# Two graph layers over a symmetric 8192x8192 adjacency on one core: second-layer parts of two adjacent rows share one step, one bank and one addition, and the finished groups are staggered

## The reference

```
x_drop  = x * (u >= 0.1) / 0.9
x       = layernorm(x + adj @ x_drop)
x_proj  = tanh(|x|) * x / (|x| + 1e-8)              # |x| clipped to 10
s       = adj @ x_proj
out     = arctanh(|s|) * s / (|s| + 1e-8)           # |s| clipped to 0.999
x       = layernorm(x + out @ kernel + bias)
```

## Time and profile before

| | |
|---|---|
| median of 3 runs | 982.45 us (981.58 to 983.51) |
| the profiled execution | 981.5 us |
| its span, first to last instruction | 979.4 us |
| mean granted TensorE clock | 0.973 |
| TensorE, VectorE, ScalarE, GpSimd busy | 92%, 38%, 5%, 6% |
| loads of blocks | 330 of 1 MB, 353.12 MB moved in all |
| chain that ended last | TensorE 78%, DMA 7%, VectorE 5%, issue 4%, GpSimd 3% |

### The profile page before, as it was taken

The page is one execution under the profiler, slowest core; times in us unless marked ns, Lnnn a source line. Parts: engine busy times, 40 slices in busy tenths (PEclk is TensorE's granted clock), DMA queues, the critical chain, the costliest instruction groups (busy, mean ns, idle before and its releaser), DMA issues.

```text
span 979.4 us, 10731 instructions
## 1 busy us (share of the span) xinstructions
PE 901.4 (92%) x4224; PEld 302.3 (31%) x4224; DVE 368.9 (38%) x1170; ACT 53.2 (5%) x138; POOL 56.9 (6%) x49
## 2 busy tenths in 40 slices
PE   5679999999999999999999999999999999999710
PEld 1113333333333333333333333333333333333210
DVE  1134683532524343423341414223060331764553
ACT  0000110000000000000000000000000000022212
POOL 0000000000000000000000000000000000022221
PEclk9999999999999999999999999999999999999955
DMA  9999999999999999999599996989989898999600
GB/s 368 413 422 421 421 420 422 421 399 417 388 394 366 418 379 421 410 399 370 229 375 421 357 362 209 416 344 373 356 308 417 311 402 332 407 419 421 261 11 22
DMA packets 52609, 353.12 MB, mean 361 GB/s; under 512 B 6224, under 2 KB 8272, under 8 KB 10320
## 3 DMA queue, kind: packets, MB, share of 16 engines
q1 hardware_dynamic: 49824, 350.25, 89.2%
q10 hardware_dynamic: 2736, 2.20, 0.7%
HBM read 350.32 MB, written 2.10 MB: 360 GB/s over the span
## 4 chain that ended last, share of the span: by engine, by line
PE 78%; DMA 7%; DVE 5%; issue 4%; POOL 3%; SPq 2%; ACT 0%; POOLq 0%; DVEq 0%
PE sums_both L596 37%; PE sums_first L560 18%; PE sums_part L560 18%; DMA ring<-adj_dram 7%; PE sums_both L578 2%; PE sums_part L578 2%; SPq L299 2%; POOL rooted L331 1%; POOL rooted L316 1%; DVE stats L409 1%; DVE y L520 1%; DVE feats L520 1%; DVE mv L412 1%; SPq L294 1%; SPq L295 0%
## 5 line engine op out<-in xcount | busy, mean ns | idle before, releaser
L596 PE MATMUL sums_both<-ring,feats 128*64 128x512 f32 x1696 | 369.9, 592 | 0.5 <-DMA ring<-adj_dram 0.5
L560 PE MATMUL sums_first<-ring,feats 128*64 128x512 f32 x1088 | 248.3, 602 | 27.4 <-DMA ring<-adj_dram 27.1
L560 PE MATMUL sums_part<-ring,feats 128*64 128x512 f32 x1088 | 237.7, 593 | 0.2 <-DMA ring<-adj_dram 0.2
L596 PEld LDWEIGHTS sums_both<-ring,feats 128*64 128x64 f32 x1696 | 121.7, 137 | 243.0 <-issue 241.0
L419 DVE TENSOR_TENSOR row_saved<-sums_both,row_saved 64x512 f32<-64x512 f32 x15 | 10.2, 683 | 337.0 <-ACT row_saved L368 337.0
L560 PEld LDWEIGHTS sums_first<-ring,feats 128*64 128x64 f32 x1088 | 76.5, 138 | 192.7 <-issue 140.9
L560 PEld LDWEIGHTS sums_part<-ring,feats 128*64 128x64 f32 x1088 | 77.5, 137 | 153.1 <-issue 151.0
L477 DVE TENSOR_TENSOR support<-sums_part,support 64x512 f32<-64x512 f32 x94 | 64.2, 683 | 103.0 <-PE sums_part L560 102.8
L326 POOL TENSOR_TENSOR rooted<-base,power 128x8 f32<-128x8 f32 x16 | 27.8, 1737 | 808.6 <-DVE base L446 808.6
L478 DVE TENSOR_TENSOR support<-sums_part,support 64x512 f32<-64x512 f32 x95 | 65.9, 694 | 3.3
L368 ACT COPY row_saved<-sums_first 64x512 f32<-64x512 f32 x16 | 9.3, 581 | 612.6 <-PE sums_first L560 612.6
(11 more groups left out here) (61 smaller groups left out, 216.7 us busy)
## 6 DMA issues: line engine op xcount, KB each, us to landing
ring<-adj_dram SPq DMA_DIRECT2D x330, 1024.0 KB, 10.9
xres<-x_dram SPq DMA_DIRECT2D x8, 256.0 KB, 16.0
support<-u_dram SPq DMA_DIRECT2D x8, 256.0 KB, 16.0
out_dram<-xres ACTq DMA_DIRECT2D x16, 128.0 KB, 4.2
selw<-selector_dram ACTq DMA_DIRECT2D x1, 32.0 KB, 3.2
selw<-weight_dram ACTq DMA_DIRECT2D x1, 32.0 KB, 3.6
bias_sb<-bias_dram ACTq DMA_DIRECT2D x1, 32.0 KB, 6.1
```

The lines of the kernel that those rows point to most:

```text
L560: last = nc.tensor.matmul(bank[at:at + F], feats[:, c * TB + t, which, :], ring[:, uses[i][0], t, :], start=start and t < 2, stop=stop and ...
L596: last = nc.tensor.matmul(sums_both[r % 2][layer * F:layer * F + F], feats[:, c * TB + t, layer, :], ring[:, slot, t, :], start=begin and ...
```

## The change

A part step now has a tuple of one or two rows, 2p and 2p + 1. For a pair, TensorE puts one row's block in the lower and the other row's block in the upper half of the bank, with the same features (`two_rows`), and one addition over 128 partitions adds both. A single row is done as before. Held columns are taken by pair where both rows hold the column; `behind` finds which rows of a pair are equally far, and rereads go by pairs. There were 95 runs of parts, all of one row; there are 51, of which 36 are of a pair. The number of second-layer cells is the same, 136 apart from those of `both` and `early`.

The tables HELD, REREAD and LEAD are others: 57 blocks are held in place of 62, and 335 are loaded in place of 330. Up to the last `turn` the order has 454 cells in place of 461 (a `both` or `early` step counts two) with 279 loads in place of 281; behind it 58 cells in place of 51.

Groups to be finished are now the pairs themselves, and the rows 4 and 5, the last, singly. FINISH_EVERY is 3 (counted in cells, at steps of mostly two). On VectorE, GpSimd and ScalarE the second half of a group's work (`residual`, `deviation`, `normalise`) stands behind the first half of the next group's, by `ended_at`; the last two groups are each done to the end.

```diff
-LEAD = 8
+LEAD = 7
-FINISH_EVERY = 6
-FINISH_LAG = 2
-HELD = [5, 5, 4, 5, 4, 5, 4, 3, 4, 6, 5, 5, 3, 2, 1, 1]
-REREAD = [0, 0, 0, 0, 0, 0, 1, 3, 3, 0, 10, 0, 5, 1, 2, 0]
+FINISH_EVERY = 3
+FINISH_LAG = 1
+HELD = [4, 4, 4, 3, 5, 4, 3, 4, 6, 5, 4, 3, 3, 2, 2, 1]
+REREAD = [0, 0, 0, 0, 0, 0, 1, 3, 3, 0, 8, 0, 4, 0, 2, 0]
...
     def column(c):
         steps = []
-        for row in range(c + 1):
-            if c < row + HELD[row]:
-                steps += partial(row, [c], True)
+        for pair in range(NB // 2):
+            rows = tuple(r for r in (2 * pair, 2 * pair + 1) if r <= c < r + HELD[r])
+            if rows:
+                steps += partial(rows, [c], True)
         return steps
+
+    def behind(pair, ready):
+
+        rows = [r for r in (2 * pair, 2 * pair + 1) if r < ready and reread_to[r] < ready]
+        low = min((reread_to[r] for r in rows), default=ready)
+        rows = tuple(r for r in rows if reread_to[r] == low)
+        others = [reread_to[r] for r in (2 * pair, 2 * pair + 1) if r not in rows and r < ready]
+        return rows, low, min([ready] + [q for q in others if q > low])
...
+    for rows, steps in groups:
+        for step in steps:
             order.append(step)
+            now += len(step[1])
+            since += len(step[1])
+            if ended and since >= FINISH_EVERY and now - ended[0][1] >= FINISH_LAG:
+                order.append(("finish", ended.pop(0)[0]))
+                since = 0
+        ended.append((rows, now))
...
+    def ended_at(k):
+
+        return ([k - 1] if 0 < k < len(groups) - 1 else []) + ([k] if k >= len(groups) - 2 else [])
...
-                    deviation(k)
+                    for late in ended_at(k):
+                        deviation(late)
...
-                    normalise(k)
+                    for late in ended_at(k):
+                        normalise(late)
...
+                if len(rows) == 2:
+                    total = support[:, rows[0] // 2]
+                    V.tensor_tensor(total, bank[:], total, ALU.add).then_inc(part_added, 1)
...
                     square_sums(k)
+                    for late in ended_at(k):
+                        if late < k:
+                            residual(late)
                     log_scale(k)
-                    residual(k)
+                    if k in ended_at(k):
+                        residual(k)
...
+            def two_rows(bank, slots, start, stop):
+
+                for t in range(TB):
+                    for g, slot in enumerate(slots):
+                        last = nc.tensor.matmul(bank[F * g:F * g + F], feats[:, c * TB + t, 1, :],
+                                                ring[:, slot, t, :],
+                                                start=start and t == 0, stop=stop and t == TB - 1)
                 return last
...
-                    two_halves(sums_part[n % PARTS], 1, i, start, stop).then_inc(block_released, 1)
+                    if len(r) == 2:
+                        last = two_rows(sums_part[n % PARTS], slots, start, stop)
+                    else:
+                        last = two_halves(sums_part[n % PARTS], 1, slot, start, stop)
+                    last.then_inc(block_released, len(r))
```

More of the change, by code:

```diff
@@ L59, in work_order, with partial @@
     reread_to = {r: r + HELD[r] for r in range(NB)}
-    def partial(row, cols, held):
+    def partial(rows, cols, held):
         nonlocal parts
         cols = list(cols)
-        steps = [("part", row, c, parts, c == cols[0], c == cols[-1], held) for c in cols]
+        steps = [("part", rows, c, parts, c == cols[0], c == cols[-1], held) for c in cols]
         parts += 1
@@ L78, in reread @@
         while budget > 0:
-            row = min(range(ready), key=lambda q: reread_to[q])
-            cols = range(reread_to[row], min(ready, reread_to[row] + budget))
-            if not cols:
+            rows, low, high = min((behind(p, ready) for p in range(NB // 2)), key=lambda q: (q[1], -len(q[0])))
+            if not rows:
                 break
-            steps += partial(row, cols, False)
-            reread_to[row] = cols.stop
-            budget -= len(cols)
+            cols = range(low, min(high, low + -(-budget // len(rows))))
+            steps += partial(rows, cols, False)
+            for r in rows:
+                reread_to[r] = cols.stop
+            budget -= len(cols) * len(rows)
         return steps
@@ L116, in work_order @@
     order += reread(LEAD, last) + column(last)
[L117 to L131, removed]
-            order.append(step)
[L133 to L147, removed]
+    pairs = sorted(range(NB // 2), key=lambda p: 2 * NB - reread_to[2 * p] - reread_to[2 * p + 1])
+    groups = []
+    for pair in pairs[:-1]:
+        steps = []
+        while True:
+            rows, low, high = behind(pair, NB)
+            if not rows:
+                break
+            steps += partial(rows, range(low, high), False)
+            for r in rows:
+                reread_to[r] = high
+        groups.append(((2 * pair, 2 * pair + 1), steps))
+    for row in (2 * pairs[-1], 2 * pairs[-1] + 1):
+        groups.append(((row,), partial((row,), range(reread_to[row], NB), False)))
+    ended, since, now = [], 0, 0
+    for rows, steps in groups:
+        for step in steps:
+            order.append(step)
+            now += len(step[1])
[4 more added lines that the diff above has]
+        ended.append((rows, now))
+    for rows, _ in ended:
+        order.append(("finish", rows))
     return order
@@ L160, in place_blocks @@
             continue
[L161 to L175, removed]
+        rows, c = step[1:3]
+        held = []
+        for r in rows if kind == "part" else (rows,):
+            if kind == "part" and step[6]:
+                slot, nth = kept.pop((r, c))
+            else:
+                n = len(loads)
+                assert n < SLOTS or n - SLOTS < len(freed), "every slot is held"
+                slot = n if n < SLOTS else freed[n - SLOTS]
+                times[slot] += 1
+                nth = times[slot]
+                loads.append((r, c, slot, max(0, n - SLOTS + 1)))
+            if kind == "hold":
+                kept[r, c] = slot, nth
+            held.append((slot, nth))
+        if kind != "hold":
+            freed += [slot for slot, _ in held]
+        uses[i] = held, len(freed)
     return loads, uses
@@ L554, in _, with two_halves @@
             finished = 0
-            def two_halves(bank, which, i, start, stop):
+            def two_halves(bank, which, slot, start, stop):
                 for t in range(TB):
@@ L568, in _ @@
                     c = step[2]
[L569 to L570 removed]
+                    slots = [slot for slot, _ in uses[i][0]]
+                    for slot, nth in uses[i][0]:
+                        pe.wait_ge(block_loaded[slot], 16 * nth)
                 if kind == "early":
@@ L605, in _ @@
                         pe.wait_ge(row_joined, r - 1)
-                    last = two_halves(sums_first[r % 2], 0, i, start, kind == "hold" and c == r)
+                    last = two_halves(sums_first[r % 2], 0, slot, start, kind == "hold" and c == r)
                     if kind == "first":
```

34 lines of the change are left out of this document (17 added, 17 removed).

## The result

The changed kernel takes 948.65 us (median of 4 runs, 946.4 to 950.22), against 982.29 us before in the same comparison: a ratio of 0.9655, 95% interval 0.9633 to 0.9677, or 3.4% less. Forecast was 946.9 us, in a range of 942.5 to 954. Its profiled execution took 946.4 us for a span of 944.2 us; 943.8 had been worked out for the span.

A forecast was written before the change was run, and what follows sets the result against it. TensorE, busy 92% of the span, bounds the kernel except in the last 55.1 us, where the finishing loop does. Saving 41.5 us there and losing 5.9 to loads gives 982.45 - 35.6 = 946.9 us, range 942.5 to 954.

The forecast's parts named there:

- The finishing loop: Two-row groups at the kernel's end: reductions follow one another after 10.5 us instead of 14.43 us.
- TensorE's wait for the loop: Behind row 15, finish 4 would start at 32.4 and must wait until 33.5, costing TensorE 1.1 us.
- After the last matmul: Only the one-row group (5,) is left behind the last block's matmuls: 13.6 us instead of 55.1, saving 41.5.
- The loads set the end of the matmuls: Last stage: the last block lands at 928.0 and its matmuls end at 930.2, costing 5.9 us; chance 0.62.
- TensorE's own end: End of the last block's matmuls by TensorE's work alone: 926.5 us, +2.2; as a rival setting the end, chance 0.13.
- 12.8 us of an earlier start: Stage behind row 15 starts 12.8 us earlier: 12.0 + 0.8.
- 18.7 us of traffic: Stage behind row 15: seven blocks and four output rows more, 7.9 MB at 421 GB/s, take 18.7 us.
- the 2.49 us a load: DMA time of one adj block of 1.049 MB, undisturbed; the five extra loads are 12.5 us of DMA.
- The additions: VectorE: 189 additions become 36 wide and 30 narrow; wide ones take 0.69 us; some 85 us go, at no gain.
- The paired matmuls: TensorE: equal weights in both halves still take 592 to 602 ns; cost 0 to 2 us, taken as 0.
- Two engines on one port: GpSimd's power beside VectorE's scale arithmetic: taken as 0; by the skill's rule the loop is about 0.8 us longer.

The follow-up runs named there:

- the run without stagger: Changed kernel with each group finished to its end before the next begins, as before the change; 966.64 us.
- the half loads: Changed kernel where the last eight loads fetch only two of a block's four tiles; 944.02 us.
- the new and the old tables: New: changed kernel with other HELD and REREAD, FINISH_EVERY 2, 944.01 us. Old: changed kernel with HELD, REREAD and LEAD of the kernel before, 953.15 us.
- the repeated run: The changed kernel itself, unaltered, run once more beside three other runs; 946.74 us.
- the unpaired run: Changed kernel with every pair step written as two runs of single rows, each with its own bank and additions; 955.57 us.

## Why the prediction was right, point by point

**The finishing loop: right.** Worked out as 10.5 us, measured 10.35. The other terms came out to 0.01 us; the residual starts at 850.52, 0.60 us behind the reduction's start, where 0.74 were counted. That the logarithm and the scale lie beside the loop is shown by the changed kernel and the run without stagger: 10.35 us with it, 14.4 without.

**TensorE's wait for the loop: right in place, 0.5 us too large.** It stands at the fifth projection, 0.64 us instead of 1.1. Two loops lie ahead of it, each 0.15 us shorter than worked out, which makes 0.3; the rest is the rounding of starts and of 8.12 to 8.1 us.

**After the last matmul: 14.1 us against 13.6.** Here a term was mis-sized. I took half of the two-row projection's 1.16 us, 0.58, for one row; from its start to the squares pass 1.19 us (931.61 to 932.80) instead of 0.68. The chain of the changed kernel, for the projection of row 4, which nothing holds up:

```profile
916.50 1.10 PE sums_first L666 x8
```

One row costs as much as two (1.09 for x16 at 839.91), so the two rows' projections, on the two halves of the partitions, run side by side, and one row alone gains nothing. That is the 0.5 us. The 0.65 us for row 4's projection ahead of the last block had the same slip and stayed hidden behind the loads. The trace of the kernel before had the sign: its one-row projection, at a granted clock of 0.50, took far more than the 1.16 us that twice 0.58 would be:

```profile
936.79 2.05 PE L629 MATMUL sums_first<-selw,support 64*128 64x128 f32 x8 [9.80 <-DVE feats L520]
```

That ScalarE would be free about 2 us early was right (2.5), and the half loads show how soon it would bind.

**The loads set the end of the matmuls: right.** 930.2 worked out, 930.10 measured; row 15 left at 815.7 against 816.0; waits in the last four cells, 2.8 us together where about 4 were named, though the distances of these cells add up to 3.6 us more than four times 1.72. The half loads give TensorE's own end: 926.0, against 926.5 worked out. The two terms that make the 930.2, 12.8 us of an earlier start and 18.7 us of traffic, were taken from the last stage's rows, not from the total of the loads. That the total does not set the time is shown by the new and the old tables: 340 loads take 944.0 us, 335 take 946.7 and 330 take 953.2. They don't test the 2.49 us a load, since other things differ too: the old tables have the fewest loads behind row 15 (47, against 52 and 56) and are slow by their finishes.

**The additions: right.** The addition over 128 partitions takes 692 ns (group of the changed kernel), against 0.69 us assumed; making it twice costs some 1 us at most by the medians.

```profile
L492 DVE TENSOR_TENSOR support<-sums_part,support 128x512 f32<-128x512 f32 x36 | 24.9, 692 | 139.2 <-PE sums_part L592 139.1
```

But "no gain" holds for VectorE's time alone. I gave no price to the order on VectorE that steps of two cells bring; undoing them, with the finishes that move along, costs 7 to 9 us. The total did not suffer, because I worked out the changed kernel's order as it stands.

**The paired matmuls: right.** Equal weights in both halves change nothing against the 592 to 602 ns of the earlier trace rows:

```profile
L592 PE MATMUL sums_part<-ring,feats 128*64 128x512 f32 x880 | 193.3, 593 | 0.0
```

**Two engines on one port: no cost seen.** The power runs beside VectorE's arithmetic in every two-row group of the staggered loop and takes 1.64 us, what it takes alone, and the product of two SBUF operands that starts within it is as long as ever:

```profile
854.33 1.64 POOL L330 TENSOR_TENSOR rooted<-base,power 128x8 f32<-128x8 f32 x1 [2.00 <-DVE minus_mean L550]
```

```profile
854.59 0.17 DVE L514 TENSOR_TENSOR norm_sq<-norm 128x8 f32<-128x8 f32 x1
```

The rule of the Trainium skill (SBUF — State Buffer, Who interferes with whom), by which one of the two waits for the whole of the other, is not borne out for operands of 8 elements a partition: VectorE's product starts 0.26 us after the power's start, 1.38 us before its end, and the loop is 10.35 us, not 11.3. No run here has long operands on both.

**Two readings of the kernel before** were loose and changed nothing. Its backlog was not seven loops of 14.43 us but six of 14.4 and one of 14.1 (the reduction at 944.76 is followed by one at 958.84). And output rows stored ahead of the last block's landing are 8 before, not 10 (the last store goes out at 914.7), and in the changed kernel 12, with two more on their way from 925.8 on; the difference of four, which the sum uses, is the measured one but for these two.

The median lies 1.75 us above the forecast, the repeated run 0.2 below; runs of the changed kernel spread over 946.0 to 950.2 us, more than the 981.3 to 983.9 of the kernel before. Why is open; nothing was tried for it.

## What to carry to other kernels

A gain at the end of a program is the sum of two things: how far the closing loop lags behind the engine that feeds it, and how much still stands behind the last piece of input. Look at each by itself; here the changes to them were worth 19 and 16 us, and they added up. Count loads by stage, not in total: the version with most loads is the fastest. In a queue that runs in order, ask of each small instruction what stands ahead of it: an addition of 1.4 us held the projection for 8.8 us, because it stood behind another group's arithmetic. And when an edit changes the size of a step, look for every rule that counts steps: undoing the pair moved the finishes as well.

## What the runs showed of the hardware that was not expected

A projection of one row, whose matmuls contract over 64 partitions, takes 1.10 us, that of two rows on both halves of the partitions 1.09: half the work saved no time.

After a wait of 6 to 11 us TensorE came back at the lower clock each time. In the run without stagger, behind the wait of 6.22 us, the stretch from 880 to 884 us has a granted clock of 0.50, which is 1.2 GHz:

```profile
880.00:884.00 4.00, 4.00 (x22) 2.03 (x20) 0.00 (x0) 2.76 (x8) 0.75 (x2) 0.50 1.02 424
```

The projection took 2.08 us in place of 1.16, and the eight cells behind it, in the timeline of the same run, 16.12 us; the changed kernel's eight took 13.95, with no long wait ahead of them:

```profile
881.49 16.12 PE L592 MATMUL sums_part<-ring,feats 128*64 128x512 f32 x64
```

```profile
874.09 13.95 PE L592 MATMUL sums_part<-ring,feats 128*64 128x512 f32 x64
```

That wait cost 3.1 us more than it lasted (0.92 + 2.17). The one of 10.63 us in the same run cost 2.4 us more (0.92, and 15.40 us for the eight cells), the one of 8.82 us of the unpaired run 2.6 us (0.92, and 10.46 us for five cells that take 8.80 with no wait ahead). Shorter waits can have it too: with FINISH_EVERY = 6 the last projection, after one projection alone and 2.75 us of waiting, ran at a granted clock of 0.50 and took 2.04 us, while that of the changed kernel, straight behind the blocks' matmuls and 1.52 us of waiting, ran at 1.00 and took 1.16.
